# A two-layer graph network: part of the second layer's sums made while the first layer still runs, and a reordered prologue and first block

## What is computed

```
h      = x @ W0 + b_W;  xi, xj = split(h)
msg(e) = xj[src e] + edge_attr e @ We + b_We
x      = layernorm(x + xi + segment_sum(msg / (in_degree + 1e-6), dst))   # layer 0
h      = x @ W1;  dinv = rsqrt(in_degree + 1)                             # layer 1, self loops added
out    = segment_sum(h[src] * dinv[src] * dinv[dst], dst) + b
y      = leaky(batchnorm(out) * gamma + beta)
result = layernorm(x + y)
```

## Time and profile before

| | us |
|---|---|
| median of three runs | 1050.24 |
| the profiled execution: its own time | 1054.36 |
| its span, first to last instruction | 1052.6 |
| TensorE busy, all of the span | 940.0 |
| VectorE busy | 688.2 |
| ScalarE busy | 475.1 |
| GpSimd busy | 349.0 |

### The profile page before, as it was taken

One profiled execution on the slowest core, in us unless ns is written; L12 is line 12 of the kernel. 1 busy time (PEld: TensorE's weight loads), 2 busy tenths in 40 slices (PEclk: granted clock), 3 DMA queues, 4 the chain that ended last, 5 costly groups with the idle time before them and its releaser, 6 DMA issues. The chain is left out here.

```text
span 1052.6 us, 32004 instructions
## 1 busy us (share of the span) xinstructions
PE 940.0 (89%) x12860; PEld 838.6 (80%) x12860; DVE 688.2 (65%) x1705; ACT 475.1 (45%) x932; POOL 349.0 (33%) x389
## 2 busy tenths in 40 slices
PE   2377998999899999999889999899999999999955
PEld 0376887888888888888778888788888888888855
DVE  3977998999999999999889999841000000000046
ACT  1434665666666666666556666551000000000037
POOL 4323454665555555556445556210000000000000
PEclk9889999999999999999999999899999999999978
DMA  7526989899999999999988999944777777777234
GB/s 152 207 106 214 331 315 379 319 367 351 356 364 334 360 355 374 327 379 334 376 301 296 344 345 363 331 160 146 302 302 282 274 294 304 297 268 282 108 101 147
DMA packets 89090, 303.79 MB, mean 289 GB/s; under 512 B 40164, under 2 KB 56760, under 8 KB 83048
## 3 DMA queue, kind: packets, MB, share of 16 engines
q1 hardware_dynamic: 86536, 296.79, 77.8%
q0 software_dynamic: 2400, 4.88, 1.4%
HBM read 219.84 MB, written 81.79 MB: 287 GB/s over the span
## 5 line engine op out<-in xcount | busy, mean ns | idle before, releaser
L867 ACT CAST counts<-pair_ps 128x800 bf16<-128x800 f32 x391 | 317.2, 827 | 209.8 <-PE pair_ps L692 208.0
L707 PE MATMUL x_ps<-counts,xsplit 128*128 128x256 bf16 (+1 forms) x2500 | 328.3, 272 | 7.6 <-issue 7.5
L476 DVE TENSOR_TENSOR lo_oh<-counter,lo_t 128x1024 bf16<-128x1024 bf16 x391 | 270.0, 690 | 27.5 <-PE pair_ps L692 27.4
L707 PEld LDWEIGHTS x_ps<-counts,xsplit 128*128 128x128 f16 x2500 | 224.1, 98 | 39.8 <-issue 18.4
L692 PE MATMUL pair_ps<-key_oh,lo_oh 128*128 128x100 bf16 x3128 | 210.6, 209 | 37.5 <-ACT counts L867 19.5
L692 PEld LDWEIGHTS pair_ps<-key_oh,lo_oh 128*128 128x128 bf16 x3128 | 182.6, 98 | 58.6 <-issue 32.0
L479 DVE TENSOR_TENSOR key_oh<-counter,key_t 128x800 bf16<-128x800 bf16 x391 | 225.6, 577 | 0.0
L669 DVE TENSOR_TENSOR xsplit<-pair_ps,dinv_row 128x256 f32<-128x256 f32 (+1 forms) x25 | 10.4, 418 | 244.0 <-PE pair_ps L776 243.3
L759 PE MATMUL pair_ps<-counts,zown 128*128 128x256 bf16 (+1 forms) x1300 | 140.5, 268 | 0.0
L759 PE MATMUL pair_ps<-streams,zown 128*128 128x256 bf16 x1200 | 135.4, 273 | 0.0
L759 PEld LDWEIGHTS pair_ps<-counts,zown 128*128 128x128 f16 x1300 | 123.0, 99 | 14.9
(11 more groups left out here) (154 smaller groups left out, 853.6 us busy)
## 6 DMA issues: line engine op xcount, KB each, us to landing
streams<-in_edge_attr SPq DMA_DIRECT2D x196, 640.0 KB
counts_kept<-counts SPq DMA_DIRECT2D x23, 3200.0 KB
streams<-counts_kept SPq DMA_DIRECT2D x12, 3200.0 KB, 12.3
counts<-counts_kept SPq DMA_DIRECT2D x11, 3200.0 KB, 12.3
dinv_row<-dinv_rows SPq DMA_DIRECT2D x25, 128.0 KB, 4.3
edst<-in_dst SPq DMA_DIRECT2D x196, 5.0 KB
counts<-in_x SPq DMA_DIRECT2D x3, 1024.0 KB, 10.2
x_rows<-x_mem SPq DMA_DIRECT2D x24, 128.0 KB
```

Of the source, the lines that this page charges most:

```text
L476: dv.tensor_tensor(lo_oh[:, at % RING, :, :, :], counter[:, :, :].unsqueeze(1).to_broadcast([P, SW // 2, P, 2]), pairs(lo_t[b % 2][:, w]). ...
L707: last = nc.tensor.matmul(x_ps[:, k % 2, 0:n], xsplit[:, q // 2, q % 2, :], by_hi[:, q // 2, :], start=(q == 0), stop=(q == 2 * HI - 1))
L867: a.copy(out.rearrange("p h (g n) -> p h g n", g=2), pair_ps[at % 2][:, :, 0:4 * KW].rearrange("p g (n h) -> p h g n", h=HI)).then_inc(S[" ...
```

## The change

**Second layer's sums.** Block k's sums over z may begin as soon as rows of z are finished. `early(k)` = 4 * (k - 1) passes, those over the source blocks 0 to k - 2, are now made in iteration k + 1 of the main part, right behind the 100 passes over x and from the same counts, into the other half of `x_ps`, so 0, 4, 8 up to 92 passes. ScalarE copies them out (`early_sums`), SP writes them to DRAM (`keep_early`, 128 KB) and reads them back in the second layer (`load_early`), where VectorE adds them to the remaining sums (`add_early`) in place of ScalarE's copy. Only the counts that are still needed are written and read. The order of blocks is now 0, 23, 24, 1, 2, ..., 22. The passes of a slot go from 7 to as many as 15 slots need.

**Update.** `offset` and `sums` come two slots earlier, `root` one later, `normalise` two later, `z_low` three later; ScalarE's `z_out` is split into two pieces in slots 11 and 12 (it was slot 8).

**Prologue and first block.** Only the first 409 heads are loaded at the start; the others are picked out by a DMA in iteration 1 and spread by another in iteration 2. Two of the three reductions `largest` come before `count_row(0)`, the third before `make_keys(0)`; `scales` and the preparation of the weights come behind the first and second one-hots of block 0. In block 0 x is turned from slot 2 on, ScalarE copies the own products (`own_out`), and GpSimd adds the bias later, one block in each iteration (`bias_own`).

The core of the diff:

```
-HEAD_PIECE = 400
...
-OWN_LAG = 5
-LOW_AT = (4, 8, 12)
+OWN_AT, HIGH_AT, LOW_AT = 2, (3, 7, 11), (6, 10, 14)
 CHUNK_ENDS = (1, 3, 7, 11, 15, 19, 22, 24, NB)
 CHUNKS = list(zip((0,) + CHUNK_ENDS, CHUNK_ENDS))
-AGAIN = [NB - 2, NB - 1] + list(range(NB - 2))
+AGAIN = [0, NB - 2, NB - 1] + list(range(1, NB - 2))
+AGAIN_AT = (2, 0, 1, 3)
...
+def early(k):
+    return 4 * max(0, k - 1)
...
             def keep_counts(k):
                 sp.wait_ge(S["pair_out"], first_slot(k) + slots(k))
-                n = HI * cols(k)
-                sp.dma_start(scratch["counts"][k * P:(k + 1) * P, 0:n], counts[k % 2][:, 0:n])\
+                at, n = early(k) // 2 * cols(k), HI * cols(k)
+                sp.dma_start(scratch["counts"][k * P:(k + 1) * P, at:n], counts[k % 2][:, at:n])\
                   .then_inc(counts_kept[k % 2], 16)
+
+            def keep_early(k):
+                sp.wait_ge(S["early_out"], early_blocks(k + 1))
+                n = cols(k)
+                sp.dma_start(scratch["sz"][:, k * BN:k * BN + n], early_sum[k % 2][:, 0:n]).then_inc(early_kept[k % 2], 16)
...
             def load_counts(i):
                 b = AGAIN[i]
-                n = HI * cols(b)
+                at, n = early(b) // 2 * cols(b), HI * cols(b)
                 if i < 4:
                     sp.wait_ge(S["e_summed"], edge_group(NB - 1, groups(NB - 1) - 1) + 1)
                 else:
                     sp.wait_ge(S["z_gathered"], i - 3)
...
-                sp.dma_start(again[i % 4][:, 0:n], scratch["counts"][b * P:(b + 1) * P, 0:n])\
+                sp.dma_start(again[AGAIN_AT[i % 4]][:, at:n], scratch["counts"][b * P:(b + 1) * P, at:n])\
                   .then_inc(counts_in[i % 4], 16)
+
+            def load_early(i):
+                b = AGAIN[i]
+                reach(sp, S["s1_ready"], i - 1)
+                sp.wait_ge(early_kept[b % 2], 16 * len(range(2 + b % 2, b + 1, 2)))
+                sp.dma_start(early_in[i % 2][:, 0:cols(b)], scratch["sz"][:, b * BN:b * BN + cols(b)])\
+                  .then_inc(early_loaded[i % 2], 16)
 
...
-                    load_counts(2)
+                    load_counts(0)
                     load_counts(3)
...
                 if i >= 4:
                     load_counts(i)
-                load_inverse(i)
+                if early(AGAIN[i]):
+                    load_early(i)
+                if i >= 2:
+                    load_inverse(i)
             for i in range(2):
+                sp.wait_ge(early_kept[i], 16 * len(range(2 + i, NB, 2)))
                 sp.wait_ge(counts_kept[i], 16 * len(range(i, NB - 2, 2)))
                 sp.wait_ge(x1_kept[i], 16 * len(range(i, NB, 2)))
...
+
+            def bias_own(b):
+                pool.wait_ge(S["weights_ready"], 1)
+                pool.wait_ge(S["own_added"], (2 * b + 1) // 4 + 1)
+                g.tensor_tensor(own[:, 2 * b:2 * b + 2, :], own[:, 2 * b:2 * b + 2, :],
+                                bi.unsqueeze(1).to_broadcast([P, 2, F]), ALU.add).then_inc(S["own_biased"], 1)
...
+                bias_own(b)
...
+            largest(0)
+            largest(1)
             for b in range(2):
                 count_row(b)
                 start_of(b)
...
+            largest(2)
             make_keys(0)
-            largest()
-            scales()
-            invert_degrees(0)
...
-                        if s in LOW_AT:
-                            split_low(LOW_AT.index(s))
+                        if s == 0:
+                            scales()
+                        if s == 1:
+                            spread_scales()
+                            ready_weights()
                         if s == 3:
                             check_rows()
-                        if s >= OWN_LAG:
...
+                    if SL * b + s in LOW_AT:
+                        split_low(LOW_AT.index(SL * b + s))
...
+            def add_early(i):
+                n = cols(AGAIN[i])
+                dve.wait_ge(S["z_gathered"], i + 1)
+                dve.wait_ge(early_loaded[i % 2], 16 * len([j for j in range(i % 2, i + 1, 2) if early(AGAIN[j])]))
+                reach(dve, S["projected"], i - 1)
+                dv.tensor_tensor(s1[i % 2][:, 0:n], z_ps[i % 2][:, 0:n], early_in[i % 2][:, 0:n], ALU.add)\
+                  .then_inc(S["s1_ready"], 1)
+
...
             for i in range(NB):
+                if i + 1 < NB and early(AGAIN[i + 1]):
+                    add_early(i + 1)
                 scale_rows(i)
                 dve.wait_ge(S["biased"], i + 1)
                 if AGAIN[i] == NB - 1:
...
-                    if q == 2 * HI - 1:
-                        last.then_inc(S["product_done"], 1)
+                passes = 2 * HI + early(k)
+                per = -(-passes // (SL - 1))
+                for q in range(min(per * (s - 1), passes), min(per * s, passes)):
+                    if k == 0 and q in [4 * first for first, _ in X_PIECES]:
+                        pe.wait_ge(S["x_low"], [4 * first for first, _ in X_PIECES].index(q) + 1)
+                    if q < 2 * HI:
+                        last = nc.tensor.matmul(x_ps[:, 0, 0:n], xsplit[:, q // 2, q % 2, :], by_hi[:, q // 2, :],
+                                                start=(q == 0), stop=(q == 2 * HI - 1))
+                        if q == 2 * HI - 1:
+                            last.then_inc(S["product_done"], 1)
+                        continue
+                    z = q - 2 * HI
+                    if z == 0:
+                        pe.wait_ge(S["z_low"], k - 1)
+                    last = nc.tensor.matmul(x_ps[:, 1, 0:n], zsplit[:, z // 2, z % 2, :], by_hi[:, z // 2, :],
+                                            start=(z == 0), stop=(z == early(k) - 1))
+                    if z == early(k) - 1:
+                        last.then_inc(S["early_done"], 1)
 
             def edges(b, g):
...
-                    if q == 0:
-                        if i >= 2:
-                            pe.wait_ge(counts_in[i % 4], 16 * len(range(i % 4 + (4 if i % 4 < 2 else 0), i + 1, 4)))
+                    if q == early(b):
+                        reach(pe, counts_in[i % 4], 16 * again_loads(i))
                         reach(pe, S["s1_ready"], i - 1)
...
-                gather_z(i, 0, 20)
+                first = early(AGAIN[i])
+                half = min(first + 20, 2 * HI)
+                gather_z(i, first, half)
                 weights(i - 1)
-                gather_z(i, 20, 2 * HI)
+                gather_z(i, half, 2 * HI)
                 add_own(i)
...
+            def early_sums(k):
+                n = cols(k)
+                act.wait_ge(S["early_done"], early_blocks(k + 1))
+                reach(act, early_kept[k % 2], 16 * len(range(2 + k % 2, k, 2)))
+                a.copy(early_sum[k % 2][:, 0:n], x_ps[:, 1, 0:n]).then_inc(S["early_out"], 1)
 
...
+            def own_out(m):
+                h, n = OWN[m]
+                act.wait_ge(S["own_done"], m + 1)
+                a.copy(own[:, h:h + n, :], j_ps[:, 0:n, :]).then_inc(S["own_added"], 1)
...
-                sums_out(i)
+                if not early(AGAIN[i]):
+                    sums_out(i)
```

More of the change, by code:

```diff
@@ L96, in first_head, with early_blocks, again_loads @@
     return max(0, min(b * BN * E // (N * HR) - HEAD_MARGIN, R - HEAD_SPAN))
+NEAR_BLOCKS = 6
+NEAR = first_head(NEAR_BLOCKS - 1) + HEAD_SPAN
+FAR = first_head(NEAR_BLOCKS)
+def early(k):
+    return 4 * max(0, k - 1)
+def early_blocks(k):
+    return sum(early(j) > 0 for j in range(k))
+def again_loads(i):
+    return i // 4 + (1 if i % 4 in (0, 3) else 0)
 class Steps:
@@ L640, in _ @@
                         edge_one_hots(b, 1)
[L641 removed]
+                    if s == 15 and 0 <= u < NB:
                         z_low(u)
[L643 to L645 removed]
             for k, n in enumerate((E, E, P * HI, P)):
@@ L759, in gather_z @@
                     nc.tensor.matmul(z_ps[i % 2][:, 0:n], zsplit[:, q // 2, q % 2, :], by_hi[:, q // 2, :],
-                                     start=(q == 0), stop=False)
+                                     start=(q == early(b)), stop=False)
             def add_own(i):
@@ L975, in sums_out @@
                 n = cols(AGAIN[i])
+                if i == 0:
+                    for k in range(2):
+                        act.wait_ge(early_kept[k], 16 * len(range(2 + k, NB, 2)))
                 act.wait_ge(S["z_gathered"], i + 1)
```

193 lines of the change are left out of this document (100 added, 93 removed).

## The result

The changed kernel takes **1093.14 us** (median of four runs, 1088.31 to 1099.62), 1.0405 times the kernel before (95% interval 1.0354 to 1.0456), which took 1050.56 beside it. The forecast was 1038, its range 1015 to 1062. The profiled execution took 1093.29 us, its span 1091.7, which is 39.1 more than before.

The account below looks back on a forecast made before the run. VectorE was taken to nearly bound the main part, TensorE alone the second layer. Terms -14 + 71.6 + 14.3 - 116.4 + 26 + 6 = -12.5 gave, from the median, 1038 us; range 1015 to 1062.

Parts of the forecast that it names:

- At nothing: The parts of the change given no cost: GpSimd's bias, the other heads, the moved update slots, the early sums' loads.
- The other heads come 20 us before use.: Prologue's remaining heads, picked and spread by later DMAs, are there 20 us before they are needed; priced at nothing.
- Prologue and block 0: Earlier first one-hots (8.5 us) and the bias leaving VectorE in block 0 (5.5): together -14 us, bounds -8 to -22.
- 22 periods and the last two iterations: Main part: passes moved there cost +71.6 us in 22 periods (bounds +63 to +101) and +14.3 in the last two iterations.
- my sum: Main part: TensorE's work added up from the timeline, 23.1 us an iteration plus 0.436 for each step of four passes.
- moves within VectorE's ring of four slots: Main part's update: moving `offset`, `sums`, `normalise` and `z_low` stays within VectorE's four slots and costs nothing.
- Passes out of the second layer and the new wait: Second layer: removed passes save 116.4 us; late loads of counts make every second gather wait, +26 (18 to 57).
- The clock: Second layer: half of the ten waits lower TensorE's clock behind them, +6 us (0 to 25).
- GpSimd's bias "1.5 us each": Main part: 25 bias additions on GpSimd, about 1.5 us each, inside iterations with room for them; priced at nothing.
- A: Rival: second layer hardly waits and the main part hides more passes, 1015 us; chance 0.18.
- B: Rival: each of ten second-layer waits costs 2.5 us of lower clock, 25 us instead of 6, 1057 us; chance 0.17.
- C: Rival: main part hides nothing, every moved pass is paid in full, +101 instead of +72, 1067 us; chance 0.10.

Follow-up runs that it names:

- e5: e1 with the picking DMA issued in iteration 0 behind `keep_inverse(0)`, where SP has a gap: 1048.74 us, 1.0073 of the kernel before.
- e1: The changed kernel with the 1223 far heads picked into SBUF, then written to DRAM as one row: 1058.63 us, 1.014 of the kernel before.
- e13: e12 with the bias taken by VectorE in block 0 again, no ScalarE copy or GpSimd addition: 1019.44 us, 0.981 of the kernel before.
- e12: e10 with ScalarE's `z_out` in slot 11 as well: 1003.06 us, 0.9641 of the kernel before.
- e10: e5 and e4 together, with a block's passes spread evenly over the 15 slots: 1009.41 us, 0.9707 of the kernel before.
- e4: e1 with VectorE scaling a place before adding the next place's early sums in the second layer: 1029.5 us, 0.9874 of the kernel before.
- e2: The changed kernel with the picking DMA, still DRAM to DRAM, issued from ScalarE at 24.6 us: 1097.95 us, 1.0513 of the kernel before.

## Why the prediction was wrong

- **The step that failed** is a half sentence under "At nothing": "The other heads come 20 us before use." It asked when the transfer's result is needed, and neither how long 1223 pieces of 4 bytes take nor what is queued behind them. The nearest row would have been the kernel before's own load of 1200 heads, which lands in SBUF in 7 us, so even that bound would have said 7; that the same pieces take over 40 us into DRAM no row showed. What rows could have told is the queue: the destinations and the write of the counts stand right behind it on SP, and the latter are what ScalarE's next block waits for. The edit had a price with an open upper end, and I gave it none; it was also no rival. It cost 46 us in the first period. e5 gives 0.033 of ratio back, some 35 us; 7 of the difference are in its second layer, where TensorE ran longer at the lower clock.
- **Prologue and block 0**, -14: -14.6 in the changed kernel and -17 to -19 in e1 and the kernels with the pick into SBUF. First one-hots at 24.63 us (26.3 forecast). The sum is near, but not its parts: I gave 8.5 to the earlier start and 5.5 to the bias, and e13 gives 16.7 to the bias and 1.3 to all else. Two errors that cancel are luck.
- **22 periods and the last two iterations**, +71.6 and +14.3: +71.4 in 21 periods (+71 in all 22 of e5) and +14.2. The first number is right by luck. With the passes even and the wait gone (e12) all 22 periods take 628.4, +57.0; so TensorE has less idle time left than I kept: e10's 30.57, 31.02 and 31.45 us stand beside 30.51, 30.95 and 31.38 of work by my sum, 0.1 idle where I had left 1.4. What filled the place of that idle time in the changed kernel was not what I had argued (`z_low` "moves within VectorE's ring of four slots" was the wrong step, as its partner on ScalarE moved by another number of slots, and I never asked how the passes are spread over the slots): 15 us in the 22 periods come from these two faults that I had not seen.
- **Passes out of the second layer and the new wait**, -116.4, +26 and +6: in sum -84.4, measured -78. (1012 x 0.110 + 92 x 0.051 is 116.0.) The wait is as argued, at every second gather at first, 1.99 to 2.99 us, the load issued about 1.5 us into the gather before; later smaller stops stand in between, and idle time is 30.8 us where I had 26. The clock took 5 us in the changed kernel (181.2 us busy for 176.0), about what I gave it, but 12 in e5 for the same idle time. e4 takes 27 us of all this away.
- **GpSimd's bias "1.5 us each"**: 2.18 in the mean, 0.73 alone and 4.15 at worst, and no cost on the path.
- **The rivals.** A, B and C are about these same terms, and all were near the forecast. The 9.5 us that A quotes come from a fit that the Trainium skill gives for DMAs issued by GpSimd; these loads are SP's, and the trace decides. The time missed the range by 31 us on a term in none of them. Without it the kernel is e5: 1.0073, still no gain, and 2% above the forecast's 0.988 (1038 by 1050). Of these 20 us e5's profile shows 13 behind `messages` of block 24: 269.8 us to the end, where the kernel before takes 340.8 and my terms 84.4 less. Of the 13, 5 are idle time above my 26 and 6 the clock above my 6. The other 7 of the 20 are of the size by which runs of the kernel before differ, and stay open.

## What to carry to other kernels

A DMA has three prices: when its result is needed, how long it holds the engines of all queues, and who stands behind it. Count its pieces and look what side they are written to, above all when it carries almost nothing. Where a step and its partner on another engine are moved, compare their distance in slots, not each one's place; and where a count is spread over slots, spread it evenly, since the fullest slot sets the pace.

## What the runs showed of the hardware

- 1223 pieces of 4 bytes from DRAM to DRAM went at 25 in a microsecond, close to 50 us in all, with 0.11 to 0.13 of the DMA engines busy. The same pieces into one partition of SBUF held the loads behind them about 6 us longer (11.3 in e1, 5.4 in e5 without pieces ahead), and in e5 2096 small packets passed in the ten microseconds from 40 us on. While the pieces into DRAM lasted, transfers of another queue slowed as well, and the pieces with them (e2). The Trainium skill, page "DMA: Bandwidth & Descriptors" (Specifications), says that below 512 bytes a DMA engine reads, changes and writes back. It gives no price for it; the runs give about 40 ns for each piece on average, and no run shows that this is the reason.
- VectorE's comparison with two inputs in SBUF grows where GpSimd's addition falls into it: up to 2.54 us, and 1.56 at most without these additions (e13). The Trainium skill, page "SBUF — State Buffer" (Who interferes with whom), says that such a VectorE instruction contends with a GpSimd one that reads SBUF, and that the order of issue decides who blocks. Here the one that began first, VectorE's at 269.27, was the one that grew, by 1.06 us, while GpSimd's took its 0.74: the trace does not bear this out for that pair. The additions of 4.15 us lie in a row of the small one-hots, which stay at 0.57 and 0.68; there the later one, GpSimd's, was the long one, and it lasted beyond the one-hot in which it began. What it waited for no run shows.
- After some stops of TensorE of 2 to 3 us its next 20 matmuls took 3.5 to 3.9 us instead of 2.39, with a granted clock of 0.60 behind the first; after others, of 2.28 and 3.31 us, they took 2.36. The length of the stop alone does not tell which.
